# Raw gates of an attention step: sums of q's and k's rows times the gate vectors on GpSimd and VectorE, in place of a product on TensorE with prepared weights

## What is computed

```python
x_norm = (x - mu) / jnp.sqrt(var + LN_EPS) * ln_w + ln_b
q = _l2norm(split_heads(x_norm @ Wq))
k = _l2norm(split_heads(x_norm @ Wk))
v = split_heads(x @ Wv)
align = jnp.einsum('bhtd,bhsd->bhts', q, k)
resonance = jax.nn.sigmoid((align - THRESH) * SHARP)
gate_q = jnp.einsum('bhtd,d->bht', q, gq)
gate_k = jnp.einsum('bhsd,d->bhs', k, gk)
modulation = resonance * gate_q[..., :, None] * gate_k[..., None, :]
collapse = jnp.einsum('bhts,bhsd->bhtd', modulation, v)
```

## Time and profile before

| what | value |
|---|---|
| median of 3 runs | 348.27 us (347.57 to 348.44) |
| the profiled execution: its own time | 347.12 us |
| its span in the profile | 345.4 us |
| PE busy | 314.2 us (91%) |
| DVE busy | 160.9 us (47%) |
| ACT busy | 89.3 us (26%) |
| POOL busy | 78.0 us (23%) |

### The profile page before, as it was taken

The page is one execution under the profiler, slowest core; times in us unless marked ns, Lnnn a source line. Parts: engine busy times, 40 slices in busy tenths (PEclk is TensorE's granted clock), DMA queues, the critical chain, the costliest instruction groups (busy, mean ns, idle before and its releaser), DMA issues. The chain is left out here.

```text
span 345.4 us, 5468 instructions
## 1 busy us (share of the span) xinstructions
PE 314.2 (91%) x1940; PEld 174.0 (50%) x1940; DVE 160.9 (47%) x349; ACT 89.3 (26%) x207; POOL 78.0 (23%) x84
## 2 busy tenths in 40 slices
PE   0998999999998899899899999999999998789992
PEld 0787667534554543454544454543475577433330
DVE  3304239463745836292858347442352647034331
ACT  1233120451213262221445411152313400011010
POOL 5000011292207000223400211321225210601212
PEclk9999999999999999999999999999999999999998
DMA  7999999999999999999496999780695043730100
GB/s 259 385 349 179 187 368 367 180 192 354 308 193 297 193 160 329 268 207 337 75 180 132 347 226 237 235 348 0 264 417 232 0 185 123 232 133 31 50 36 9
DMA packets 61221, 74.29 MB, mean 215 GB/s; under 512 B 3174, under 2 KB 40070, under 8 KB 60176
## 3 DMA queue, kind: packets, MB, share of 16 engines
q1 hardware_dynamic: 59648, 69.23, 77.6%
q0 software_dynamic: 1552, 4.78, 3.9%
HBM read 70.85 MB, written 3.67 MB: 216 GB/s over the span
## 5 line engine op out<-in xcount | busy, mean ns | idle before, releaser
L792 DVE STREAM_TRANSPOSE CT_sb<-FF_sb 128x1024 f32<-128x1024 f32 x36 | 42.4, 1220 | 14.2 <-DMA FF_sb<-ctx 12.6
L1194 PE MATMUL ST<-CTX_sb,PR_sb 128*64 128x512 f32 (+1 forms) x208 | 47.7, 599 | 1.1 <-ACT PR_sb L339 1.1
L1169 PE MATMUL SC<-CT_sb,qcurP_sb 128*64 128x256 f32 x288 | 37.6, 388 | 1.6 <-DVE CT_sb L792 0.8
L1194 PEld LDWEIGHTS ST<-CTX_sb,PR_sb 128*64 128x64 f32 (+1 forms) x208 | 14.1, 136 | 24.3 <-issue 23.5
L1169 PEld LDWEIGHTS SC<-CT_sb,qcurP_sb 128*64 128x64 f32 x288 | 18.6, 136 | 15.0 <-issue 7.5
L1094 PE MATMUL A<-AW_sb,normT_sb 128*128 128x512 f32 x48 | 22.0, 600 | 0.0
L518 POOL TENSOR_TENSOR rn_sb<-ss_sb,nhalf_sb 128x16 f32<-128x16 f32 x4 | 11.6, 2906 | 36.5 <-DVE ss_sb L871 36.5
L1087 PE MATMUL TR<-ident_sb,CTX_sb 128*128 128x128 f32 (+1 forms) x128 | 16.1, 266 | 1.8 <-DVE CT_sb L332 1.1
L1087 PEld LDWEIGHTS TR<-ident_sb,CTX_sb 128*128 128x128 f32 (+1 forms) x128 | 12.9, 141 | 8.3 <-issue 5.6
L1114 PE MATMUL A<-AW_sb,WQK_sb 128*128 128x256 f32 x64 | 16.2, 417 | 0.8 <-ACT AW_sb L603 0.8
L1344 PE MATMUL SC<-ident_sb 128*128 128x128 f32 x130 | 16.4, 278 | 0.0
(11 more groups left out here) (242 smaller groups left out, 487.7 us busy)
## 6 DMA issues: line engine op xcount, KB each, us to landing
CTX_sb<-ctx SPq DMA_DIRECT2D x24, 1024.0 KB, 10.8
FF_sb<-ctx SPq DMA_DIRECT2D x80, 128.0 KB, 7.1
FF_sb<-ctx SPq DMA_DIRECT2D x32, 256.0 KB, 8.1
CTX_sb<-wgu SPq DMA_DIRECT2D x4, 1024.0 KB, 9.5
CTX_sb<-wdn SPq DMA_DIRECT2D x5, 512.0 KB, 12.3
FF_sb<-wgu SPq DMA_DIRECT2D x2, 1024.0 KB, 6.3
rows<-XR_sb SPq DMA_DIRECT2D x3, 512.0 KB, 10.5
CTX_sb<-ctx SPq DMA_DIRECT2D x8, 130.0 KB
```

Of the source, the lines that this page charges most:

```text
L792: v.transpose(ctxT[:, pos % 2, k, :, :].rearrange("p c (b r) -> p b c r", r=Q), split[:, k, at:at + BLOCKS, :].rearrange("p b (c r) -> p b ...
L1169: last = t_.matmul(out[q, :], (qcurP if split_group else qcur)[:, c, q], ctxT[:, pos % 2, k, c, 0:n], start=(c == 0), stop=(c == DC - 1))
L1194: last = t_.matmul(ST[q, :], probs[0:w, t, q], ctxb[0:w, k, t, :], start=(t == 0), stop=(t == KT - 1))
```

## The change

The step "graw" is gone, and with it the preparation of `wgate`. The raw gates come from the rows themselves:

- POOL, in step "k": between the two powers it multiplies `kh` with the vector `gk` into the first half of `res` (`kg`), and behind the second power `qh` with `gq` into the second half of `res` (`qg`). As `qh` is already divided by its norm, its sum needs no factor.
- DVE, in step "turn": it sums `kg` by head into `graw` and multiplies by k's norm. In step "align0", behind its scaling, it sums `qg` straight into the gates of q. Its scaling of the second half in "align1" comes behind that sum, since it writes over `qg`.
- ACT: the spreading of q's gate moves from step "turn" to behind the tanh of "align0".

```diff
-STEPS = ("sum", "on", "y", "stats", "norm", "a2", "v", "q", "graw", "k", "kT", "turn", ...
+STEPS = ("sum", "on", "y", "stats", "norm", "a2", "v", "q", "k", "kT", "turn", ...
...
+        kg, qg = (res[:, 2 * i:2 * i + 2, :].rearrange("p c (j d) -> p (c j) d", d=HD) for i in range(2))
...
                 elif step == "k":
+
+                    earlier(pool, "resbd_made", 4 * p)
+                    pool.wait_ge(s["k_moved"], p + 1)
+                    g.tensor_tensor(kg, kh[:, :].rearrange("p (h d) -> p h d", h=HEADS),
+                                    rowv[:, 2 * D + HD:].unsqueeze(1).to_broadcast([P, HEADS, HD]), ALU.mult).then_inc(s["kg_made"], 1)
                     pool.wait_ge(s["ssk"], p + 1)
                     g.tensor_tensor(rn[:, HEADS:], ss[:, HEADS:], nhalf[:, HEADS:], ALU.pow).then_inc(s["powk"], 1)
+                    pool.wait_ge(s["qh_made"], p + 1)
+                    g.tensor_tensor(qg, qh[:, :].rearrange("p (h d) -> p h d", h=HEADS),
+                                    rowv[:, 2 * D:2 * D + HD].unsqueeze(1).to_broadcast([P, HEADS, HD]), ALU.mult).then_inc(s["qg_made"], 1)
...
-            for n in range(2 * DC):
...
-                g.tensor_tensor((sq, kh)[n % 2][:, :].rearrange("p (h d) -> p h d", h=HEADS), w, gv, ALU.mult).then_inc(s["gmul"], 1)
...
-                    act.wait_ge(s["gates_made"], p + 1)
-                    a.copy(gq.rearrange("p (h d) -> p h d", h=HEADS),
-                           gates[:, 0:HEADS].unsqueeze(2).to_broadcast([P, HEADS, HD])).then_inc(s["gq_made"], 1)
...
+                    if half == 0:
+                        act.wait_ge(s["qg_sum"], p + 1)
+                        a.copy(gq.rearrange("p (h d) -> p h d", h=HEADS),
+                               gates[:, 0:HEADS].unsqueeze(2).to_broadcast([P, HEADS, HD])).then_inc(s["gq_made"], 1)
...
+                    dve.wait_ge(s["kg_made"], p + 1)
+                    link(v.tensor_reduce(graw[:], kg, AX.X, ALU.add))
                     dve.wait_ge(s["powk"], p + 1)
-                    dve.wait_ge(s["graw_moved"], p + 1)
-                    v.tensor_tensor(gates[:], graw[:], rn[:], ALU.mult).then_inc(s["gates_made"], 1)
+                    v.tensor_tensor(gates[:, HEADS:], graw[:], rn[:, HEADS:], ALU.mult).then_inc(s["gates_made"], 1)
...
+                    if half == 1:
+                        dve.wait_ge(s["qg_sum"], p + 1)
...
+                    if half == 0:
+
+                        dve.wait_ge(s["qg_made"], p + 1)
+                        v.tensor_reduce(gates[:, 0:HEADS], qg, AX.X, ALU.add).then_inc(s["qg_sum"], 1)
...
-            gate_sums(0, 2)
...
-                elif step == "graw":
-                    pe.wait_ge(s["gred"], 2 * DC)
-                    for c in range(DC):
-                        last = t_.matmul(ST[:, 0:2 * HEADS], normT[:, c, :], wgate[:, c, :], start=(c == 0), stop=(c == DC - 1))
-                    last.then_inc(s["graw_made"], 1)
```

More of the change, by code:

```diff
@@ L68 @@
 ROWV = 2 * D + 2 * HD
-STEPS = ("sum", "on", "y", "stats", "norm", "a2", "v", "q", "graw", "k", "kT", "turn", "align0", "align1", "bd", "gT", "col", "o",
+STEPS = ("sum", "on", "y", "stats", "norm", "a2", "v", "q", "k", "kT", "turn", "align0", "align1", "bd", "gT", "col", "o",
          "hnorm", "h", "route", "rank")
-BY_SCORES = {0: ("sum",), 1: ("on",), 2: ("y",), 3: ("stats",), 4: ("norm",), 5: ("a2",), 6: ("v", "q", "graw", "k"), 7: ("kT",),
+BY_SCORES = {0: ("sum",), 1: ("on",), 2: ("y",), 3: ("stats",), 4: ("norm",), 5: ("a2",), 6: ("v", "q", "k"), 7: ("kT",),
              8: ("turn",), 9: ("align0",), 10: ("align1",), 11: ("bd", "gT"), 12: ("col",)}
@@ L84 @@
 BY_SUMS = {1: ("hnorm", "h"), 2: ("route",), 3: ("rank",)}
-LAST_SCORES = {0: ("sum",), 1: ("on",), 2: ("y",), 3: ("stats",), 4: ("norm",), 5: ("a2",), 6: ("v",), 8: ("q", "graw")}
+LAST_SCORES = {0: ("sum",), 1: ("on",), 2: ("y",), 3: ("stats",), 4: ("norm",), 5: ("a2",), 6: ("v",), 8: ("q",)}
 LAST_MAX = ("k",)
@@ L91 @@
 ENDING = ((_L, "sum"), (_B, "align0"), (_L, "on"), (_B, "align1"), (_B, "bd"), (_L, "y"), (_L, "stats"), (_B, "gT"),
-          (_B, "col"), (_L, "norm"), (_L, "a2"), (_L, "q"), (_L, "graw"), (_L, "k"), (_L, "v"), (_L, "kT"), (_L, "turn"),
+          (_B, "col"), (_L, "norm"), (_L, "a2"), (_L, "q"), (_L, "k"), (_L, "v"), (_L, "kT"), (_L, "turn"),
           (_L, "align0"), (_L, "align1"), (_L, "bd"), (_B, "o"), (_L, "gT"), (_L, "col"), (_B, "hnorm"), (_L, "o"),
@@ L101 @@
 AFTER = dict(zip(STEPS, STEPS[1:] + ("end",)))
-LINKS = {"sum": 1, "stats": 2, "q": 1, "k": 1, "o": 2, "route": 5, "rank": 2}
+LINKS = {"sum": 1, "stats": 2, "q": 1, "k": 1, "turn": 1, "o": 2, "route": 5, "rank": 2}
 LINK_AT = {}
@@ L182, in program @@
         res = sb("res", [P, DC, HPC * S])
+        kg, qg = (res[:, 2 * i:2 * i + 2, :].rearrange("p c (j d) -> p (c j) d", d=HD) for i in range(2))
         XR_own = sb("XR", [P, 2 * D])
         XR_l = CT[:, NT * P + 4 * D:NT * P + 6 * D]
-        wgate = sb("wgate", [P, DC, 2 * HEADS])
         gwT = sb("gwT", [P, DC, E])
@@ L268, in program @@
             a2_made ratio_made a2_turned rawT_made normT_made v_made v_moved q_made q_sq ssq powq qh_made
-            k_made k_sq ssk powk k_moved graw_made graw_moved gates_made vp_made q_turned qmask_act qmask_dve
+            k_made k_sq ssk powk k_moved gates_made vp_made q_turned qmask_act qmask_dve
             k_turned kT_made al_made scaled_made res_made resbd_made col_made gq_made gq_turned gqT_made cgT_made
@@ L673, in attention @@
                     a.activation(sq, A0[:, :], ACT.Square).then_inc(s["k_sq"], 1)
-                elif step == "graw":
-                    act.wait_ge(s["graw_made"], p + 1)
-                    a.copy(graw[:], ST[:, 0:2 * HEADS]).then_inc(s["graw_moved"], 1)
                 elif step == "kT":
@@ L965, in _ @@
             shift(0)
-            def gate_sums(m, n):
-                for i in range(m, n):
-                    dve.wait_ge(s["gmul"], i + 1)
-                    at = HEADS * (i // DC)
-                    v.tensor_reduce(wgate[:, i % DC, at:at + HEADS], (sq, kh)[i % 2][:, :].rearrange("p (h d) -> p h d", h=HEADS),
-                                    AX.X, ALU.add).then_inc(s["gred"], 1)
-            gate_sums(0, 2)
             move_numerators(dve, v.tensor_copy, 0, 1)
-            gate_sums(2, 6)
             turn_split(1, NEXT.groups[0])
-            gate_sums(6, 2 * DC)
             move_numerators(dve, v.tensor_copy, 0, 3)
@@ L1163, in score @@
                     if grp == GROUPS - 1:
-                        earlier(pe, "graw_moved", p)
+                        earlier(pe, "on_made", p)
                 out = SC[:, lo * P:lo * P + n] if grp < GROUPS - 1 else ST[:, 0:n]
```

19 lines of the change are left out of this document (6 added, 13 removed).

## The result

The changed kernel takes 352.36 us (median of 9 executions, 349.51 to 353.83) against 348.57 (347.18 to 352.48) for the kernel before in the same session: a ratio of 1.0102, 95% interval 1.0059 to 1.0145. The direction was forecast, the size was not: 350.0, at most 351.2. One execution of either kernel lies up to 4 us off its median, so a single profile is read here for its parts, not for its total; the ratios leave disturbed executions out, the pooled table further down has them all. The profile after is of an execution of 352.77 us, 5.65 above the profiled execution of before; its span is 351.0, 5.6 above.

What follows compares the result with a forecast made beforehand. PE, busy for 91% of the span, was taken to bound the kernel; 0.64 + 1.35 + 0 + 0.54 - 0.81 = +1.72 on the median 348.27 gave 350.0 us, range 347.9 to 351.2.

Steps and rivals of the forecast that it cites:

- the wait at "gT": PE, turning the spread gate in each loop turn, waits for DVE's second scaling; forecast to grow to 1.5 us or more.
- Second turn, +1.35: Loop's second turn: DVE's second scaling and "gT" come later by 0.75 from held gates plus 0.60 from qg's sum.
- Gates held by qg: Loop turns: DVE's small gate product, both inputs in SBUF, waits until POOL's qg multiplication ends; 0.75 in the second turn.
- The row of L942: DVE's similar product, 166 ns three times and 380 once beside POOL's copy; read as waiting for POOL's instruction to end.
- The rival without a hold: Loop turns: DVE's gate product gets through beside qg or costs only 0.2 more; sum +0.2 (+0.4), chance 0.24.
- First turn, 1.63 - 0.99 = +0.64: Loop's first turn: 1.03 for held gates plus 0.60 for the sum, less 0.99 of PE's later waits as slack.
- the first turn's slack is not there: Rival: the transfer awaited in the first turn lands later, so the 0.99 is lost too; +2.7, 351.0, chance 0.14.
- Preparation, nothing: Removing eight POOL multiplications and eight DVE sums that prepared wgate gains nothing; at most 0.24.
- Last turn, 0: Last turn: PE's 0.63 wait for DVE's turning only grows by what the removed product saves, so 0.
- Ending, +0.54 and -0.81: Ending: ACT's gate spreading delays the copy PE's projection awaits, +0.54; pair 3's removed product saves 0.81.
- kg hidden: POOL, between the two powers in the second turn: the kg multiplication, 1.27 us, is hidden with 0.35 to spare.

Runs made afterwards that it cites:

- filled: Changed kernel with six unused matmuls ahead of "gT" in each loop turn, one variant also with the preparation put back unused; pooled mean 351.42 us.
- E5: Kernel before, plus POOL's multiplication of qh behind k's power in the loop turns, result unused, second scaling behind it; 349.56 us, one execution.
- E6: Kernel before, plus a DVE sum of qh into a spare between the two scalings in the loop turns; 347.72 us, one execution.
- E1: Changed kernel with k's raw gates written to PSUM in the two loop turns; 348.76 us, ratio 1.0010 to the kernel before.
- C1: Changed kernel repeated unchanged for a second profile; 353.16 us, ratio 1.0165 to the kernel before.
- E3: Changed kernel with six unused matmuls on PE ahead of "gT" in each loop turn; 351.04 us, ratio 1.0115 to the kernel before.
- G2: Same kernel as E3 (changed kernel, six unused matmuls ahead of "gT"), run in another session; 351.83 us, ratio 1.0114 to the kernel before.
- E7: Kernel before with the new way for pair 3 alone, the product and preparation kept for the other pairs; 347.27 us, ratio 0.9965.
- C0: Kernel before repeated unchanged for a second profile; 348.38 us, ratio 0.9974.
- E2: Changed kernel with POOL's multiplication qg moved behind its multiplication of v; 350.94 us, ratio 1.0115 to the kernel before.
- G1: Changed kernel with the six unused matmuls ahead of "gT" and the removed preparation put back, its result unused; 351.85 us, ratio 1.0115 to the kernel before.
- E8: Kernel before with both POOL's unused multiplication of qh and DVE's unused sum between the scalings, in the loop turns; 351.59 us, one execution.

## Why the prediction was wrong in size

The direction, the hold and most terms stood. **The step that failed is the one behind the wait at "gT"**: the forecast put the wait at 1.5 us or more and charged only the delay itself. What the clock does behind such a wait was no term of the sum; the traces show 1.0 us of it in each turn of the first profile. **A second step is short as well**: what the change costs ahead of the second turn, +0.64 for the first turn and nothing for the preparation. With the clock kept up, the time is still 2.9 over before and not 1.7, and by the sum below some 1.8 of it lies there; which of the two terms has it stays open. By term:

- **Second turn, +1.35.** The waiting cost 1.40 (59.06 less 0.98 of clock; 58.08 when filled). Right to 0.05. Its parts: E5's hold and E6's sum, less what the earlier k projection gives back (E1 pays 0.31 where E6 pays 0.59).
- **The clock, no term.** 1.0 us in each turn of the first profile, 1.1 and 2.0 in C1. With it the second turn came to +2.38 and +3.45.
- **Gates held by qg.** Right, in both turns: 1.16 and 1.09 us, ending 0.03 behind POOL's instruction each time; 0.17 with one operand in PSUM or with POOL elsewhere. The row of L942 had been read rightly. The rival without a hold is out. The Trainium skill, "SBUF — State Buffer", section "Who interferes with whom", has this rule, and its other half too, that a DVE instruction with at most one SBUF input (outside its two-port modes) does not contend; E1 agrees, with 0.17.
- **First turn, 1.63 - 0.99 = +0.64.** Mis-sized, as far as the times go. In the first profile the delay was +1.91 (q to gT; +1.30 in E3, +2.76 in G2, the same kernel), and 1.02 of slack was used up behind it (23.19 to 22.17), so the credit of 0.99 was there. It was there in every profile of a kernel whose loop is unchanged: against the shortest, 21.91, the stretch from "o" to "y" had 1.3 us in the kernel before, 1.1 in E7, and some 2.2 in C0, its fall of the clock taken off. E6, with at most 0.6 of delay put ahead of it, had none left, so it is not always that large. But over many executions the filled kernel is 2.9 ± 0.4 over before; its second turn explains 1.40 and its ending -0.32, which leaves 1.8 for all that lies ahead of the second turn. As a number that is nearer to the rival "the first turn's slack is not there" (+2.7 in all), whose mechanism the traces do not show. The profiles can't settle it: from the first turn's "y" to the second's it is 59.42, 62.11 and 58.89 us in the kernel before, C0 and E7, and 59.58, 62.61 and 60.51 in E3, G2 and G1. E2 doesn't fit in: by the same working all ahead of its second turn would cost 1.7 (± 0.6), with gates that are free. In its one profile PE waited 1.98 us there for a context transfer and lost the clock behind it, which may be chance.
- **Preparation, nothing.** Wrong by 0.25 at least, and perhaps by more. With the slack used up, the kernels with the preparation (G1, E5, E6, E8) show 21.91 or 21.92 from "o" to "y", all seven without it 22.17 or 22.18: 0.25 us, which PE waits longer for ACT ahead of "y" (0.66 in E3, 0.41 in G1). A larger effect, through the transfer awaited ahead of the first turn, is neither shown nor excluded (G1 and G2).
- **Last turn, 0.** Right: 0.63 to 1.44, exactly the saving.
- **Ending, +0.54 and -0.81.** +0.52 and -0.92, with another 0.08 lost beside it. Right.
- **kg hidden.** Right: powk waited 0.36 us for DVE's sum of squares behind it, not for kg.

With the first turn at its full 1.63 and 0.25 more for the preparation, the sum would be 1.88 + 1.40 - 0.32 = +3.0, against the 2.9 of the filled kernels; with the clock's 2.1 (by the pulses) it would be 5.1, against 4.1 ± 0.5 for the changed kernel in the table. The first sum fits, but it was made after the fact, and no run shows that the 0.99 is lost. **Still open**: what the fall of the clock costs in time, how the part ahead of the second turn splits between the hold, the preparation and the transfers, and why the clock does not fall behind every such wait.

## What to carry to other kernels

Where a small DVE product reads two SBUF operands, ask what POOL does at that moment. Here 0.17 us became 1.1, and putting one operand in PSUM took it back; the kernel was then as fast as before, within what can be told (1.0010, 0.9974 to 1.0047). And when a forecast makes PE's wait longer, add a term for the clock behind it as a chance, not only the wait. A slack that rests on the landing of a transfer in one profile is no credit until a second profile of the same kernel shows it.
